# Block 2's attention: the next sequence's row maxima sent in two halves of eight heads instead of all at once

## The reference

```python
x = L0_attn_x
xn = _layernorm(x, axis=-1)
s = _L0_attn_ref(xn, ...)
g = _silu(_L0_ffn_ref(xn, ...))
x = x + s * g
xn = _layernorm(x, axis=-1)
s = _L1_attn_ref(xn, ...)
g = _silu(_L1_ffn_ref(xn, ...))
x = x + s * g

def _L1_attn_ref(hidden_states, w_qkv, b_qkv, w_proj, b_proj):
    ...
    scores = jnp.einsum('bqhd,bkhd->bhqk', q, k) * scale
    ...
    bias = slopes[:, None, None] * rel[None, :, :]
    causal = pos[None, :] <= pos[:, None]
    scores = jnp.where(causal[None, None], scores + bias[None], jnp.finfo(scores.dtype).min)
    attn = jax.nn.softmax(scores, axis=-1)
    out = jnp.einsum('bhqk,bkhd->bqhd', attn, v).reshape(B, S, H)
    return out @ w_proj + b_proj
```

## Time and profile before

| | us |
|---|---|
| median of three runs (684.63 to 689.01) | 685.59 |
| the profiled execution | 689.09 |
| its span, from the first to the last instruction | 686.4 |

### The profile page before, as it was taken

One profiled execution on the slowest core, in us unless ns is written; L12 is line 12 of the kernel. 1 busy time (PEld: TensorE's weight loads), 2 busy tenths in 40 slices (PEclk: granted clock), 3 DMA queues, 4 the chain that ended last, 5 costly groups with the idle time before them and its releaser, 6 DMA issues.

```text
span 686.4 us, 12626 instructions
## 1 busy us (share of the span) xinstructions
PE 612.2 (89%) x4114; PEld 480.5 (70%) x4114; DVE 401.8 (59%) x972; ACT 319.6 (47%) x698; POOL 204.0 (30%) x228
## 2 busy tenths in 40 slices
PE   4989998999999999998777979997978769999994
PEld 4868887899988888777455646665656547787663
DVE  6376657555545384757684766563534156666577
ACT  2213334566554334433354434543434458888542
POOL 0237540300005450400220003452456505555400
PEclk9999999999999999999989999999899989999998
DMA  9995563643325320351559526646730304554363
GB/s 320 273 62 171 164 209 96 204 119 116 110 70 181 72 62 1 112 138 30 130 158 211 114 80 174 154 154 181 141 70 3 50 18 142 162 159 140 111 213 106
DMA packets 90167, 88.85 MB, mean 129 GB/s; under 512 B 31407, under 2 KB 82690, under 8 KB 88290
## 3 DMA queue, kind: packets, MB, share of 16 engines
q1 hardware_dynamic: 81706, 69.14, 39.9%
q0 software_dynamic: 7888, 18.79, 8.8%
q10 hardware_dynamic: 512, 0.13, 0.1%
HBM read 51.44 MB, written 36.45 MB: 128 GB/s over the span
## 4 chain that ended last, share of the span: by engine, by line
PE 72%; DVE 15%; DMA 5%; issue 3%; ACT 3%; SPq 1%; POOL 0%; ACTq 0%; DVEq 0%; POOLq 0%
PE bank L925 10%; PE bank L1004 9%; PE bank L1036 6%; PE bank L757 5%; PE bank L1085 4%; PE bank L990 3%; PE bank L1142 3%; PE bank L850 3%; PE bank L945 3%; PE bank L1160 3%; PE bank L1117 3%; PE bank L1017 3%; DMA QS<-mT 2%; PE bank L802 2%; PE bank L1144 2%
## 5 line engine op out<-in xcount | busy, mean ns | idle before, releaser
L646 POOL DMA_INDIRECT slots<-xn,slot_of x64 | 66.1, 1032 | 133.8 <-DVE slot_of L1817 61.8
L2038 DVE TENSOR_REDUCE mneg<-bank 128x2 f32<-128x512 f32 (+1 forms) x96 | 62.6, 685 | 50.4 <-PE bank L1119 49.8
L670 POOL DMA_INDIRECT rets<-results,slot_of x32 | 34.2, 1070 | 108.8 <-DMA results<-ys 69.7
L743 POOL DMA_INDIRECT results_by_token<-ys,logits x47 | 45.5, 967 | 51.2 <-ACT ys L1486 49.9
L1942 DVE TENSOR_TENSOR xgl<-bank,xgh 128x256 f16<-128x256 f32 (+1 forms) x86 | 36.4, 424 | 38.5 <-ACT xgh L1463 37.9
L1568 ACT ACTIVATE exps_first_keys<-bank 128x512 f32<-128x512 f32 x64 | 35.2, 597 | 41.5 <-PE bank L1144 41.3
L1914 DVE TENSOR_TENSOR hf<-bank,sg 128x512 f32<-128x512 f32 x36 | 24.8, 688 | 47.4 <-PE bank L925 47.4
L1142 PE MATMUL bank<-QS,KS 101*128 101x256 bf16 (+1 forms) x256 | 37.7, 263 | 15.0 <-DMA QS<-mT 14.6
L1438 ACT ACTIVATE sg<-bank 128x512 f32<-128x512 f32 x36 | 21.5, 598 | 61.2 <-PE bank L925 61.2
L1117 PE MATMUL bank<-KS,QS 99*128 99x256 bf16 (+1 forms) x256 | 38.4, 259 | 10.4 <-DVE mneg L2038 9.4
L1949 DVE TENSOR_TENSOR hs<-bank,gs 128x176 f32<-128x176 f32 x86 | 29.3, 341 | 26.9 <-ACT gs L1469 23.7
(11 more groups left out here) (236 smaller groups left out, 1633.9 us busy)
## 6 DMA issues: line engine op xcount, KB each, us to landing
xn<-slots SPq DMA_DIRECT2D x86, 128.0 KB, 2.2
projection_parts<-parts SPq DMA_DIRECT2D x8, 768.0 KB, 3.9
QS<-projection_parts SPq DMA_DIRECT2D x16, 384.0 KB
KS<-projection_parts SPq DMA_DIRECT2D x16, 384.0 KB
slots<-zrow SPq DMA_DIRECT2D x1, 6016.0 KB, 27.1
results<-ys SPq DMA_DIRECT2D x39, 128.0 KB, 1.7
x<-in_x SPq DMA_DIRECT2D x8, 512.0 KB, 6.2
rets<-results_by_token SPq DMA_DIRECT2D x8, 512.0 KB, 7.0
```

The costliest lines, as they stand in the source:

```text
L646: pool.indirect_dma_start(out=slots_dram, out_offset=bass.IndirectOffsetOnAxis(ap=at, axis=0), in_=xn[:, t, :], in_offset=None).then_inc(s ...
L743: pool.indirect_dma_start(out=returned_dram, out_offset=bass.IndirectOffsetOnAxis(ap=returns_to[:, j:j + 1], axis=0), in_=ys1[:, j % YRING ...
L2038: dve.tensor_reduce(mneg[:, qt, first:first + 2 * heads - 1:2], PS[6 + p % 2][:].rearrange("p (n k) -> p n k", n=heads), AX.X, ALU.max, ne ...
```

## The change

`mT` gets a second half. In each unit with a next sequence, the first eight heads' maxima (scores 0 to 5) are transposed, split and sent after `weighted_values(u, 1)`, and the other eight where all sixteen were sent before. `scores_T(u, 0)` waits for the first half, `scores_T(u, 2)` for the second. The transposes take half as many columns of `mneg` each, so there are four per sequence in place of two; DVE has four operations in place of two, and ACT issues four DMAs of 4 KB in place of two of 8 KB. Bank 7 holds the transposed maxima in the middle of the unit too, so score 7, which writes that bank, waits until DVE has read them. ACT issues each half only when the half before it has landed. Sequence 0 sends both halves together.

```diff
-        mT = sb("mT", [2 * 32, SEQ], BF16)
+        mT = sb("mT", [2 * 32, 2, SEQ], BF16)
...
                 elif p == 1:
-                    pe.wait_ge(mt_sb, after(bb))
+                    pe.wait_ge(mt_sb, after(2 * bb))
+                elif p == 7:
+                    pe.wait_ge(sm_read, after(12 * bb + 6))
+                    if bb:
+                        pe.wait_ge(mt_sb, after(2 * bb + 1))
                 else:
...
-            def max_transposes(bb):
-                pe.wait_ge(sm_read, after(12 * bb + 12))
-                for qt in range(2):
-                    mm = pe.transpose(PS[MAX_BANK][0:32, qt * P:(qt + 1) * P], mneg[:, qt, :], ident)
-                mm.then_inc(mt_ps, 1)
+            def max_transposes(bb, sides):
+                pe.wait_ge(sm_read, after(12 * bb + 6 * sides.stop))
+                for side in sides:
+                    for qt in range(2):
+                        mm = pe.transpose(PS[MAX_BANK][0:H // 2, side * SEQ + qt * P:side * SEQ + (qt + 1) * P],
+                                          mneg[:, qt, side:H:2], ident)
+                mm.then_inc(mt_ps, len(sides))
...
-                if g == 0:
-                    pe.wait_ge(max_landed, 32 * (bb + 1))
+                if g % 2 == 0:
+                    pe.wait_ge(max_landed, both_halves(bb) + 32 * (g // 2 + 1) if bb else both_halves(1))
...
                 if now:
                     weighted_values(u, 1)
+                if ahead:
+                    max_transposes(u + 1, FIRST)
                 if done:
                     outputs_transposes(u - 1)
...
-                    max_transposes(u + 1)
+                    max_transposes(u + 1, SECOND)
...
-            def place_maxima(bb):
-
-                act.wait_ge(mt_sb, after(bb + 1))
-                for part in range(2):
-                    row = MAX_ROW + part
-                    act.dma_start(QS[bb % 3][row:row + 1], mT[32 * part:32 * part + H, :])\
-                       .then_inc(max_landed, 16)
+            def place_maxima(bb, sides):
+
+                act.wait_ge(mt_sb, after(2 * bb + sides.stop))
+                if bb:
+                    act.wait_ge(max_landed, both_halves(bb) + 32 * sides.start)
+                for side in sides:
+                    for part in range(2):
+                        row = MAX_ROW + part
+                        act.dma_start(QS[bb % 3][row:row + 1, side:H:2, :], mT[32 * part:32 * part + H // 2, side, :])\
+                           .then_inc(max_landed, 16)
...
                 if u == 0:
                     x_copies(1, NCH - 1, (0,))
+                if ahead:
+                    place_maxima(u + 1, FIRST)
                 sums_copy(u, 0)
                 exp_scores(u, 3)
...
-            def read_max(bb):
-
-                src = PS[MAX_BANK][0:32, 0:SEQ]
-                dve.wait_ge(mt_ps, after(bb + 1))
+            def read_max(bb, sides):
+
+                src = PS[MAX_BANK][0:H // 2, sides.start * SEQ:sides.stop * SEQ].rearrange("p (s n) -> p s n", n=SEQ)
+                high, low = (mT[r:r + H // 2, sides.start:sides.stop, :] for r in (0, 32))
+                dve.wait_ge(mt_ps, after(2 * bb + sides.stop))
...
                 if ahead:
+                    read_max(u + 1, FIRST)
                     for p in (7, 8):
                         maxima(u + 1, p)
```

More of the change, by code:

```diff
@@ L115, in column, with both_halves @@
     return 2 * (h % 8) + h // 8
+FIRST, SECOND, BOTH = range(0, 1), range(1, 2), range(0, 2)
+def both_halves(sequences):
+    return 64 * sequences
 def prime(eng, sems):
@@ L547, in load_sequence @@
                 if bb >= 2:
-                    sp.wait_ge(max_landed, 32 * (bb - 1))
+                    sp.wait_ge(max_landed, both_halves(bb - 1))
                 if bb >= 3:
@@ L1234, in _ @@
                 project(j, BOUNDARY_BANK[j])
-            max_transposes(0)
+            max_transposes(0, BOTH)
             front(1, NCH - 2)
@@ L1627, in attention @@
                 if ahead:
-                    place_maxima(u + 1)
+                    place_maxima(u + 1, SECOND)
                     if j is None:
@@ L1640, in _ @@
             mid_part(4)
-            place_maxima(0)
+            place_maxima(0, BOTH)
             x_copies(1, NCH - 2)
@@ L2039, in maxima @@
                                   AX.X, ALU.max, negate=True).then_inc(sm_read, 1)
-            def read_max(bb):
-                src = PS[MAX_BANK][0:32, 0:SEQ]
-                dve.wait_ge(mt_ps, after(bb + 1))
+            def read_max(bb, sides):
+                src = PS[MAX_BANK][0:H // 2, sides.start * SEQ:sides.stop * SEQ].rearrange("p (s n) -> p s n", n=SEQ)
+                high, low = (mT[r:r + H // 2, sides.start:sides.stop, :] for r in (0, 32))
+                dve.wait_ge(mt_ps, after(2 * bb + sides.stop))
                 if bb:
[L2046 to L2049, removed]
+                    dve.wait_ge(max_landed, both_halves(bb - 1) + 32 * sides.stop if bb > 1 else both_halves(1))
+                dve.tensor_copy(high, src).then_inc(mt_high, len(sides))
+                dve.wait_ge(mt_high, after(2 * bb + sides.stop))
+                dve.tensor_tensor(low, src, high, ALU.subtract).then_inc(mt_sb, len(sides))
             def first_maxima(k):
@@ L2139, in _ @@
             sums(1, NCH - 2, front1)
-            read_max(0)
+            read_max(0, BOTH)
             rest_part(4, BOUNDARY_BANK[4])
@@ L2215, in attention @@
                     maxima(u + 1, 11)
-                    read_max(u + 1)
+                    read_max(u + 1, SECOND)
                     if j is not None:
```

## The result

| | before | after |
|---|---|---|
| median, us | 688.22 (20 runs, 682.35 to 693.77) | 681.37 (20 runs, 673.89 to 686.98) |
| ratio, 95% interval | 1 | 0.9866 [0.9843, 0.9889] |
| profiled execution, its span | 689.09, 686.4 | 685.43, 683.7 |

Both kernels ran on the same chip. The ratio is some 9.2 us; forecast were 9.7. It leaves out five of the changed kernel's twenty executions as slow ones (684.42 us and more, the profiled one among them); by the medians of all twenty the gain is 6.9 us, a ratio of 0.990. In time, 681.37 us stand against a forecast of 675.9; 2.6 us of the difference come from the base, for which the forecast took 685.59, the median of three runs. The profiled execution of the changed kernel is 4.1 us above the median, and the profile says where its time went.

What follows compares the result with a forecast made beforehand. PE was taken to bound the kernel, with 14.6 us of waits for maxima, mostly at units' starts, and slow clock behind some. Gains 14.8 less costs 5.1 gave net -9.7 us: 675.9 us against the 685.59 median, range 672 to 684.

Steps and rivals of the forecast that it cites:

- The wait, its size and its clock: Starts of units: PE's wait for maxima goes, 14.6 us, plus slow clock behind it; near 19 us at most, 14.8 taken.
- Unit 1: Start of unit 1: DVE's first maxima are late next, so 3.0 us come in of 3.82 us and the slow clock.
- the prediction's own signs of being wrong: PE waiting at scores_T(u, 2), at score 7 for line 2049's operation, or at weighted_values(u, 3) for exponentials.
- Unit 0: Unit 0: ACT's issues delay the second half of x's copy, so PE's router waits; cost 1.0 us (0 to 1.3).
- Transposes: PE, seven units: two more transposes per sequence, 0.4 us a pair, on the path; cost 2.8 us.
- Sequence 0: Ahead of unit 0: 0.4 us more transposes and 0.5 for DVE's wider operations, unhidden; cost rounded to 1.0 us.
- the second half: At scores_T(u, 2): the second half lands in time, 1.9 us to spare in unit 5, 1.0 in unit 6; costed at nothing.
- ACT in units 1 to 7: Middle of units: two more issues of 0.61 us on ACT stay hidden, 2 us to spare before weighted_values(u, 3).
- Behind the units nothing else is late: After the units: POOL's clearing of dn_second still leaves 3 us before ACT needs it, with the units 9.7 us earlier.
- The wait at a unit's start: Rival: the wait returns at unit 5 (load) and unit 6 (second half), 3.3 us less gain, 679.2 us; chance 0.16.
- the hand-over in unit 1: Rival, for all seven units: mid-unit hand-over makes PE wait 0.6 us before score 7, 4.2 us, 680 us; chance 0.10.
- the issue overhead in unit 0: Rival, for all units: overhead of further issues comes through, 9.8 us less 1.0 already counted, 684.7 us; chance 0.06.

Runs made afterwards that it cites:

- the scatter alone: Changed kernel with POOL's second scatter waiting after every 8 transfers in place of 4, without the other edits: ratio 0.9889 to the kernel before.
- the four issues: Changed kernel with the first half placed by four issues of 2 KB in place of two of 4 KB: ratio 0.9925 to the kernel before.
- sequence 0's maxima moved: Changed kernel with sequence 0's maxima copied behind the normalisation on DVE and placed behind x's copies on ACT: ratio 0.9828 to the kernel before.
- unit 0's order mended: Changed kernel with ACT issuing the first half behind the second copy of x, in unit 0 alone: ratio 0.982 to the kernel before.

## Why the prediction was right, and where its steps were not

**The wait, its size and its clock: right.** Units 5 and 6 gave 4.7 and 6.2 us net of the transposes where 4.0 and 5.8 were forecast, unit 7 its 1.2. In unit 5 the load of sequence 6 is next in line, as said: a wait of 1.43 us (forecast 2.0), and 0 to 2.77 in the variants that keep the early half. It is the least steady unit of theirs, 19.0 to 24.6 us, also because the clock fell to 0.50 behind that wait in two of them (2.15 and 2.77 us) and stayed at 1.00 behind 1.43, 1.93 and 2.71. At the starts of the units it stayed at 1.00 in the changed kernel.

**Unit 1: the step failed.** "Of 3.82 us and the slow clock only 3.0 us come in" was right at its place: DVE's first maxima came 10.06 us after the end of unit 0 before (380.26 less 370.2) and 6.80 after. But only 0.8 us were left at the unit's end. DVE then held PE by 1.81 us at a later score, and the low clock moved behind that wait:

```profile
386.87 0.39 PE L1129 MATMUL bank<-KS,QS 99*128 99x256 bf16 x2 [1.81 <-DVE mneg L2059]
...
395.40 0.38 PE L1129 MATMUL bank<-KS,QS 99*128 99x256 bf16 x2 [0.53 <-DVE mT L2071]
```

```profile
386.00:388.00 2.00, 1.13 (x11) 0.86 (x15) 2.00 (x4) 0.00 (x0) 0.00 (x0) 0.97 1.14 279
388.00:390.00 2.00, 2.00 (x21) 1.13 (x14) 1.93 (x19) 0.02 (x1) 0.00 (x0) 0.50 0.85 139
390.00:392.00 2.00, 2.00 (x16) 1.39 (x14) 0.16 (x2) 1.71 (x3) 0.00 (x0) 0.68 0.42 107
```

DVE's idle time ahead of the next maxima (at 391.92) is 1.84 us for 0.23 before, 1.6 us lost. The hand-over at score 7 cost the other part: from maximum 5 to maximum 7 DVE took 4.01 us (391.92 to 395.93) against 3.23, so 0.8, the upper bound, where 0.3 was taken. 3.26 - 1.61 - 0.78 is the 0.9 that is left. The other profiles with the early half bear this out: all have the wait of 1.81 us, the clock fell behind it in six of the eight, and they took 27.5 to 27.7 us; in the two where it stayed at 1.00 (the scatter alone, the four issues) unit 1 took 25.9 and 26.0, some 2.4 less than the 28.4 before, where 2.3 was forecast. So DVE's part was right, and the term left out is the clock behind DVE's wait. PE waiting at score 7 for the new line 2049 (0.53 us) was also one of the prediction's own signs of being wrong; it showed in this unit alone.

**Unit 0: the mechanism was right, the size was not.** The router's wait is 0.94 us for 1.0 forecast. The term that was too small is what stands behind that wait: the values at low clock, 1.7 us more. The prediction counted the clock where a wait was removed and not where one was added.

**Transposes: right in kind, too large.** 0.39 us a pair as said, but units 2 to 4 grew by 0.5 us together and not by 1.2, and doubling a pair showed 0.2 to 0.3. Part of it falls into waits for maxima that PE has anyway.

**Sequence 0, the second half, ACT in units 1 to 7: right.** Sequence 0 gave +1.0 us: the transposes took 0.60 for 0.38, each of DVE's operations 0.68 for 0.41. The stage differs by as much between executions of the same code (12.9 to 14.0 us with the change, 11.9 and 13.2 without), with the clock; compared at like clock the change costs 0.7 to 1.0. No profile has a wait at `scores_T(u, 2)` for the second half or one for the last exponentials.

**"Behind the units nothing else is late": failed in the profiled execution, held in others.** POOL's work starts from its first scatter and not from the units' ends, as the text said, but the 3 us to spare were taken from one execution. The chain varies by 8 us (117.4 to 125.3), and with the units' end earlier it is sometimes late and sometimes not. In the twelve profiles the stretch to the experts is 23.3 to 23.6 us where POOL is on time and the last output's matmuls keep their clock, up to 25.0 where only the clock falls, as before, and 28.0 to 29.2 in the three where POOL is late. The clock in this stretch was no term of the prediction.

**The rivals.** The wait at a unit's start (for the load in unit 5), the hand-over in unit 1 and the issue overhead in unit 0 each came in at one place; none of the three in all units. The Trainium skill's rule to coalesce small transfers (DMA: Bandwidth & Descriptors, Rules for kernel authors) agrees with the price: an issue takes 0.61 us at 8 KB, 0.63 at 4 KB and 0.60 at 2 KB. By the runs this price is paid where ACT stands in PE's way, which is unit 0. Two more issues per unit showed elsewhere only in unit 5, where the half was issued beside the load, and cost nothing there on balance.

The total was near because errors cancelled: unit 0 and unit 1 came out 3.5 us dearer together, and units 2 to 6 1.8 us cheaper. That is luck. By the profile's stages it leaves -8.0 us; the runs say -9.2, with an interval of some 1.6 us on either side, and -6.9 by the medians of all.

## What to carry to other kernels

Splitting a hand-over so that its first part leaves early pays in those units whose next wait is far behind; look for what is next in each, since a unit that another engine fills (unit 1) gives the gain back inside the unit. Price a new wait with the clock behind it, as one does a removed one. Before comparing a stage of two profiles, compare the granted clock in it: unit 1 seemed to gain 0.4 us from the wait and gained 2 at like clock. Where a transfer chain on another queue doesn't move with the change, compare its spread over executions, not one value, with the time to spare.

## Unexpected behaviour of the hardware

**One DVE operation takes three times as long beside one of POOL's.** Of the four normalisations of `xn` ahead of unit 0 one took 1.24 us and the others 0.40. It ended (near 339.8) just behind POOL's operation of 338.42 + 1.23 = 339.65. In the run with sequence 0's maxima moved, POOL's came after the four, and none took longer than 0.41. All twelve profiles agree: in the eight where POOL's operation begins just ahead of the fourth, the kernel before among them, the fourth takes 1.24 us; in the four where it begins behind it, 0.41 at most. DVE's rows of `xn` (ns, minimum/median/maximum), then POOL's timeline, of the changed kernel:

```profile
L1757 DVE TENSOR_SCALAR xn<-x,mv,rs x4: 402/402/1237, 337.6 to 338.6; 128x256 f32<-128x256 f32 x4
```

```profile
338.42 1.23 POOL L726 TENSOR_TENSOR parts<-rest,parts 128x512 bf16<-128x512 f32 x1 [4.98 <-ACT parts L1539]
```

And of the run with the maxima moved:

```profile
L1757 DVE TENSOR_SCALAR xn<-x,mv,rs x4: 404/407/409, 333.7 to 334.6; 128x256 f32<-128x256 f32 x4
```

```profile
335.27 1.16 POOL L726 TENSOR_TENSOR parts<-rest,parts 128x512 bf16<-128x512 f32 x1 [2.51 <-ACT parts L1539]
```

That is 0.84 us of the 3.8 that the moved step gained, and it can't be read from either engine's rows alone. The Trainium skill (SBUF — State Buffer, SBUF: two separate sides) describes the ports that these two engines share as an exclusive lock, held for a whole instruction; the rows agree with it.

**A wait of under 1 us can cost the clock.** Behind 0.94 and 0.32 us of waiting around the router's sixteen small matmuls the granted clock was 0.50 (1.2 GHz) from 372 to 374, where behind 1.68 us ahead of unit 7 it had stayed at 1.00. The 0.32 alone didn't do it: with unit 0's order mended it is still there, and the values ran at 1.00.
